# Layer 1 of a four-layer kernel: queries, keys and query mask one unit sooner, and a new order at the start

## What is computed

```python
x = x + _L0_xattn_ref(_layernorm(x, axis=-1), ctx_4096, Wq, bq, Wk, bk, Wv, bv, Wo, bo)
x = x + _L0_ffn_ref(_layernorm(x, axis=-1), ...)
x = x + _L1_xattn_ref(_layernorm(x, axis=-1), ctx_4096, ...)
...
```

```python
q = _pointwise(Wq, bq, x); k = _pointwise(Wk, bk, cond); v = _pointwise(Wv, bv, cond)
k_win = pad(k)[:, :, idx]; v_win = pad(v)[:, :, idx]
dots = jnp.einsum('bhdt,bhdtw->bhtw', qh, k_win) * hd ** -0.5
out = jnp.einsum('bhtw,bhdtw->bhdt', softmax(dots), v_win)
return _pointwise(Wo, bo, out)
```

## Time and profile before

| | |
|---|---|
| Median of three runs | 1677.43 us (1676.12 to 1679.34) |
| The profiled execution's own time | 1670.39 us |
| Its span, first to last instruction | 1668.6 us |
| TensorE busy | 1565.1 us (94%) |
| DVE, ACT, POOL busy | 822.3, 754.2, 516.7 us |
| Mean granted TensorE clock | 0.989 |

### The profile page before, as it was taken

One profiled execution on the slowest core, in us unless ns is written; L12 is line 12 of the kernel. 1 busy time (PEld: TensorE's weight loads), 2 busy tenths in 40 slices (PEclk: granted clock), 3 DMA queues, 4 the chain that ended last, 5 costly groups with the idle time before them and its releaser, 6 DMA issues. The chain is left out here.

```text
span 1668.6 us, 25980 instructions
## 1 busy us (share of the span) xinstructions
PE 1565.1 (94%) x9522; PEld 1276.6 (77%) x9522; DVE 822.3 (49%) x1697; ACT 754.2 (45%) x2529; POOL 516.7 (31%) x648
## 2 busy tenths in 40 slices
PE   6988998789999999999999998878999999999998
PEld 4877776678888888888888887655555578888876
DVE  4556655455444455554444435765565422343454
ACT  3445453445454454454454555444343211454552
POOL 5766654232222221222221223333232100123423
PEclk9999999999999999999999999998999999999999
DMA  8000000102001010101010110001100000222101
GB/s 237 15 7 8 7 1 14 51 1 95 26 20 45 1 39 26 39 26 39 26 39 26 39 51 1 1 29 51 38 1 1 20 9 15 65 77 72 50 27 60
DMA packets 45678, 58.22 MB, mean 35 GB/s; under 512 B 26368, under 2 KB 33920, under 8 KB 42736
## 3 DMA queue, kind: packets, MB, share of 16 engines
q1 hardware_dynamic: 43872, 56.05, 10.6%
q10 hardware_dynamic: 1616, 0.51, 0.1%
q0 software_dynamic: 64, 0.00, 0.0%
HBM read 48.94 MB, written 2.10 MB: 31 GB/s over the span
## 5 line engine op out<-in xcount | busy, mean ns | idle before, releaser
L1728 ACT ACTIVATE big<-pb 128x128 f32<-128x128 f32 x384 | 106.6, 277 | 315.3 <-PE pb L795 206.0
L2090 POOL TENSOR_TENSOR big<-big 128x512 f32<-128x512 f32 x96 | 99.9, 1041 | 261.2 <-DVE big L1378 261.2
L1779 ACT ACTIVATE big<-pb,big 128x128 f32<-128x128 f32 x384 | 135.8, 367 | 65.1 <-issue 42.0
L1373 DVE TENSOR_REDUCE big<-pb 128x4 f32<-128x512 f32 x96 | 65.9, 686 | 178.9 <-PE pb L834 170.7
L810 PE MATMUL pb<-wkh,CXh 128*128 128x256 f32 x512 | 149.3, 292 | 1.5 <-DVE big L1363 1.5
L2080 POOL TENSOR_SCALAR big<-big 128x6 f32<-128x6 f32 x64 | 13.0, 203 | 425.0 <-ACT big L1728 424.7
L810 PE MATMUL pb<-wkl,CXh 128*128 128x256 f32 x512 | 144.3, 282 | 0.0
L810 PE MATMUL pb<-wkh,CXl 128*128 128x256 f32 x512 | 143.6, 281 | 0.0
L1168 DVE TENSOR_TENSOR X<-X,pb 128x512 f32<-128x512 f32 x128 | 86.9, 679 | 86.3 <-PE pb L1016 41.5
L859 PE MATMUL pb<-woh,oh 128*128 128x512 f32 x256 | 111.8, 437 | 8.0 <-DVE X L1168 5.0
L795 PE MATMUL pb<-wqh,CXh 128*128 128x512 f32 x256 | 103.1, 403 | 10.9 <-DVE wql L1194 5.1
(11 more groups left out here) (256 smaller groups left out, 3958.5 us busy)
## 6 DMA issues: line engine op xcount, KB each, us to landing
big<-in_w SPq DMA_DIRECT2D x17, 1024.0 KB, 4.9
big<-in_w SPq DMA_DIRECT2D x24, 256.0 KB, 3.0
big<-in_w SPq DMA_DIRECT2D x8, 512.0 KB, 3.5
o<-o SPq DMA_DIRECT2D x96, 32.0 KB, 1.9
X<-in_x SPq DMA_DIRECT2D x8, 256.0 KB, 5.3
big<-in_cn SPq DMA_DIRECT2D x8, 256.0 KB, 2.7
CXlf<-in_cT SPq DMA_DIRECT2D x8, 256.0 KB, 5.2
big<-in_wa SPq DMA_DIRECT2D x1, 2048.0 KB, 8.1
```

The costliest lines, as they stand in the source:

```text
L1373: v.tensor_reduce(m[j % 2], quarters(bank(p)), AX, MAX, negate=True).then_inc(S.m, 1)
L1728: y = a.activation(sq[i % 2], bank(p)[:, j * width:j * width + 128], ACT.Square, accum_out=ss[i % 2][:, first + j:first + j + 1])
L1779: y = a.activation(e_[:, c], bank(p)[:, c], ACT.Exp, bias=m[j % 2][:, k:k + 1], scale=1.0, accum_out=z[j % 2][:, k:k + 1])
L2090: g.tensor_tensor(quarters(e_), quarters(e_), bc(r[j % 2], 128), MUL).then_inc(*on.to(S.pn))
```

## The change

1. In `l0`, a new stage `l0_qk` (delay 1, last in the step) makes queries and keys, which were part of `l0_project` (delay 2, in the middle). It carries TensorE's L683 and L687 and ACT's L1636 and L1643.
2. POOL's query mask is a stage `l0_mask`, delay 2 as before, but first in the step, ahead of the scaling of the probabilities.
3. `l0_rows` keeps delay 1 and becomes first in the step.
4. `begin` is taken apart. The loads on ACT's queue are in another order on five semaphores, and each user waits for its own. DVE clears only the 8-column edges of `CPt`; the identity's cast and the bias product become a stage `l0_bias` after step 2. SP's first context load waits for nothing.
5. `l1_begin` stands inside step 35, ahead of that step's down matmul and first norm, instead of behind it.
6. The places of `ffn0` in a step are renumbered, and are the same between the same stages; the values in waits on `S.zero` follow the new count of clears.

```diff
-    l0 = [("l0_sum", 4), ("l0_out", 7), ("l0_weigh", 6), ("l0_turn", 5), ("l0_scores", 3), ("l0_project", 2),
-          ("l0_rows", 1), ("l0_norm", 0)]
+    l0 = [("l0_mask", 2), ("l0_rows", 1), ("l0_sum", 4), ("l0_out", 7), ("l0_weigh", 6), ("l0_turn", 5),
+          ("l0_scores", 3), ("l0_project", 2), ("l0_norm", 0), ("l0_qk", 1)]
...
-        together(next(att0), (ffn0, 4), (ffn0, 7))
-    order.append(("l1_begin", 0))
+        if step == 4 * NT + 3:
+            together(next(att0), (iter([[("l1_begin", 0)]]), 6), (ffn0, 6), (ffn0, 8))
+        else:
+            together(next(att0), (ffn0, 6), (ffn0, 8))
+        if step == 2:
+            order.append(("l0_bias", 0))
...
             def begin(_):
-                on.wait_ge(D.ident, 16)
-                v.tensor_copy(identb[:, :], ident[:, :]).then_inc(S.zero, 1)
-                v.memset(CPt[0], 0.0).then_inc(S.zero, 1)
-                v.memset(CPt[1], 0.0).then_inc(S.zero, 1)
+                for k in range(2):
+                    v.memset(view(CPt[k], 0, [[520, 2], [1, 8]]), 0.0).then_inc(S.zero, 1)
                 v.memset(Kbd[0], 0.0).then_inc(S.zero, 1)
                 v.memset(Kbd[1], 0.0).then_inc(S.zero, 1)
                 v.memset(mg, -MAGIC).then_inc(S.zero, 1)
                 v.memset(mgp, MAGIC).then_inc(S.zero, 1)
-                p = PSUM["begin", 0, "bo"]
+
+            def l0_bias(_):
+                on.wait_ge(D.ident, 16)
+                v.tensor_copy(identb[:, :], ident[:, :]).then_inc(S.zero, 1)
+                p = PSUM["l0_bias", 0, "bo"]
...
-                for dst, name in ((wq0, "wq0"), (wk0, "wk0"), (wv0, "wv0"), (wob, "wo0"), (bq0, "bq0"), (bk0, "bk0"),
-                                  (bo0, "bo0"), (bv0, "bv0"), (hm, "hm"), (hmo, "hmo"), (pad, "pad"), (band[0:16], "band")):
-                    a.dma_start(dst, d[name]).then_inc(D.w0, 16)
-                on.wait_ge(D.w0, 192)
+                for dst, name, landed in ((wq0, "wq0", D.wqk), (bq0, "bq0", D.wqk), (wk0, "wk0", D.wqk), (bk0, "bk0", D.wqk),
+                                          (band[0:16], "band", D.band), (wv0, "wv0", D.wv), (pad, "pad", D.wv),
+                                          (hm, "hm", D.hm), (bv0, "bv0", D.wo), (wob, "wo0", D.wo), (bo0, "bo0", D.wo),
+                                          (hmo, "hmo", D.wo)):
+                    a.dma_start(dst, d[name]).then_inc(landed, 16)
+                on.wait_ge(D.band, 16)
+                a.copy(bandb[0:16], band[0:16]).then_inc(S.band, 1)
...
                 load(ident[:, :], d["ident"], D.ident)
-                on.wait_ge(S.zero, 3)
                 load_cn(0)
```

## The result

The change took 1669.12 us (median of 15 runs, 1666.14 to 1674.73); the kernel before, run beside it, 1676.97 us (15 runs). The ratio of the means is 0.9963, 95% interval 0.995 to 0.9976: 6.2 us faster. The prediction said 14.25 us. It had the sign right, and the time lies in its range, but the gain is less than half of the forecast.

A forecast was written before the change was run, and what follows sets the result against it. TensorE, 90% busy or more over most of the span, leaves time only in the first block's waits. Terms -5.5 - 11.0 + 8.75 - 6.0 - 2.7 + 2.2 = -14.25 us, from 1677.43 to 1663.2 us; range 1655 to 1674.

The forecast's parts named there:

- The start: Before 20 us: X's first tile and DVE's clears let queries and first scores come 7.0 to 4.8 us sooner; -5.5 us.
- The stated bound of 0: Start's other limit: no gain if POOL's instruction ahead of the first L1980 fills all 7.67 us that hide it.
- Rival 1: At the start, POOL's unseen instruction keeps the first `rs` at 12.4, losing all 5.5 us: 1668.7 us; chance 0.30.
- The mask: Scores' waits for POOL's mask, 11.0 us in 7 waits between 20 and 300 us, go: -11.0 us.
- little gets past the next gate: After the mask: DVE waits for `rs` and its later out hold the gate, so little of the mask's gain remains.
- the 5 us that it would cost if queries held bank 4: Weigh waits up to 0.7 us a tile for the queries' copy to free bank 4; left out of the sum.
- Queries and keys sooner: ACT's copies move a step earlier, so the turn's waits for L1694 (five tiles, 6.5 us) go: -6.0 us.
- The rows at the head: DVE waits for the reciprocal root before sum and out, delaying five gates by 1.75 us each: +8.75 us.
- Rival 2: DVE's out stays on time, the 8.75 shrink to 3 and clock loss to -2.9: 1652.4 us; chance 0.12.
- Rival 3: Rows' wait at DVE's queue head sets the step's pace, 4.4 us per gate, 22 in all: 1684.7 us; chance 0.07.
- `l1_begin`: Earlier `wql` subtractions bring the second attention's first matmul from 298.3 to 295.5: -2.7 us, bounds -5.1 and 0.
- The clock: TensorE's slow stretches follow waits: three gates go slow, +5.1, the stretch at 221 us goes, -2.9: +2.2 us.

The follow-up runs named there:

- Holding SP: The change, with SP issuing nothing after the first context tile until ACT's last four loads have landed: 1659.35 us, ratio 0.9908 to the kernel before.
- the order alone: The change with the old loads, clears, semaphore and bias, DVE waiting for the identity before its clears: 1668.62 us, ratio 0.9958 to the kernel before.
- both series: Two series of the unedited change against the kernel before: 1669.12 us, ratio 0.9963, and again 1669.46 us, ratio 0.9974.
- the order alone, with SP held and not: Old start in the new order; SP's loads held by DVE's wait for the identity, 1668.62 us, or released at 2 us, 1673.88 us.

## Why the prediction was half right

**The start, -5.5: wrong, 0 measured.** This is the step that failed. It priced the landing of X's first tile (3.1 to 5.3 us) and put ACT's loads of weights and biases, which the queries wait for as well, at nothing: "ACT is ready for them: its issues end at 6.03 + 0.45." It saw that "SP's context load and all behind it now go out beside ACT's" and let that move the value only within its range. The crowd took `bk` to 7.3 us and `hmo` to 8.3, and ACT's issues ended at 9.0: 1.5 us were won by the first scores instead of 5.5, and the spell at 1.2 GHz behind them took 5.2. Holding SP brought the first scores to 12.2 us, inside the forecast 11.9 to 14.1. The stated bound of 0 was right, its cause was another: "The bias product waits for four loads, but stands behind the first values" overlooked that these four are last in the crowd, and that the scores stand behind it in TensorE's queue.

**Rival 1, POOL's unseen instruction: refuted.** The first L1999 stands at 4.75 us, 0.30 behind its operand. The rule of the Trainium skill, GPSIMD Engine Reference, section Instruction dispatch (about 6 us at the first call of a freshly loaded kernel) finds no such gap in this profile. Rival 1's price came true by another cause.

**The mask, -11.0: its wait went, but not all of it was won.** The wait is gone from the profile. Where TensorE used to wait 2.15 us for it, it now comes sooner to the next norm's turning (L656, 1.5 us in all, none before), to the up rows' quantization (L666, 2.5, none before) and to the weigh (5.3 and 0.4, 3.0 before). These give back 6.7 us, for which the sum has no term; "little gets past the next gate" thought of DVE alone. The prediction took L1680 for the second quantization and called that late next, by about 0.1 us; it waits once, 1.58 us before and after. And the 5 us that it would cost if queries held bank 4 are 0.4 in the profile (L746 for L1655), rightly left out; the 5.3 are a wait for ACT's copies (L1713). The new waits, and a weigh above 4 us, are in every profile with the new order and in none with the old. No run moved the mask without the queries, so how the 6.7 divide between the two is read from the timeline and not shown.

**Queries and keys sooner, -6.0: right as to its own wait.** The turn's 6.5 us are gone.

**The rows at the head, +8.75: about right.** Forecast 1.75 us for each of five gates; those of steps 13, 17, 21, 25 and 29 wait 0.46, 1.56, 1.55, 1.56 and 2.23 us longer, 7.3 in sum, and taking the rows away from the head gave back 9 to 11 us, slow gates included. Rival 2 falls with it. Rival 3 does not come about: three gates lost 1.6 to 2.2 by the wait and 1.7 by the clock, none 4.4.

**`l1_begin`, -2.7: too high.** Measured 1.8 and 1.3. The wait for `wql` turned into one of 2.5 us of the out for L1330, as drawn.

**The clock, +2.2: right in the profiles, open in the times.** It forecast that three of the four gates behind scores 16, 20, 24 and 28 go slow and that the slow stretch at 221 us goes. So it is: in the profile after, the gates of steps 21, 25 and 29 took 5.41 us, 3 x 1.7 more, as did that of step 33, which was slow before too; and L722 at 224.28 took 2.00. The windows show it as 0.94 of the clock at 120 to 300 us, 0.96 before. But over the runs the mean clock of the change (0.984 in both series) is that of before (0.984 beside the second), so that its net price doesn't show in the times.

The four terms of waits were forecast at -11.0 + 8.75 - 6.0 - 2.7 = -10.95 and measured at -7.8 in the change's profile, -5.9 in that of the order alone. With the clock's 2.2 the order part was forecast at -8.75, and the order alone gained 7.0 us (interval 4.5 to 9.7): this part holds within the noise, with the missing 6.7 partly made up by terms that came out better. What remains between 14.25 and the change's 4.4 to 6.2 us is the start. Rival 4 said that terms of the sum are waits whose place another takes; of the mask's 11.0 that is true.

## What to carry to other kernels

When a wait or a clear that held one queue back is removed, price the loads of the other queues again: a landing time read while that queue was silent is no bound for when it isn't. Let the few small loads that the first work needs go first, and hold the bulk until they have landed. In an engine's in-order queue, put an instruction that waits for another engine behind those that someone waits for: one stage's place was worth 9 to 11 us here, without any change in the work. And when a wait is taken away, look for the next producer that the engine will now meet sooner.

## What the runs showed of the hardware that was not expected

A load of 512 bytes landed 2.7 us after its issue beside a held queue and 7.3 us beside 256 KB loads; one of 2 KB took 1.9 and 8.3. With the same order of loads on ACT's queue the pairs are 2.5 and 5.8, and 2.0 and 5.9 (the order alone, with SP held and not). An issue on ACT took up to 1.95 us in the crowd, 0.45 outside it.

TensorE's first large products are slow whatever the start. The first queries and keys took 2.08 and 1.86 us in the kernel before, at 13.63 and 15.50; the next ones, at 34.99, took 1.08 and 1.02. The windows view has a granted clock of 1.00 over 0 to 15 us all the same, so at the start the durations tell more than that figure.

TensorE fell to its lower clock soon after the sooner, interrupted start: idle until 9.43 us, 5 us of work, 2.5 us idle, then 1.2 GHz from 17 us. The start of before, idle until 13.63 but for one small product and then without such a gap, kept 1.00 to 40 us, as did both kernels with the order alone. Holding SP gave 0.95 and 1.00 in two profiles and 0.78 and 0.79 in two others, with nearly the same first 12 us and no wait of TensorE over 0.7 us from there to 20. What decides it stays open; at 5 us a time it is as large as the terms that were argued over.
